# A decoder layer's banded self-attention: the row of maxima copied by ScalarE, and GpSimd's division three steps later

## The reference

```python
scores = jnp.einsum('bhtd,bhsd->bhts', q, k) / SCALE
scores = jnp.where(causal[None, None], scores, NEG_INF)
attn = jax.nn.softmax(scores, axis=-1)
mask = jnp.clip((R + z[:, :, None, None] - dist) / R, 0.0, 1.0)
attn = attn * mask
attn = attn / (attn.sum(axis=-1, keepdims=True) + 1e-08)
out = jnp.einsum('bhts,bhsd->bhtd', attn, v)
```

## Time and profile before

| what | value |
|---|---|
| device time, median of 3 runs | 3279.68 us (3276.38 to 3284.31) |
| the profiled execution | 3284.68 us |
| its span, first to last instruction | 3282.8 us |
| mean granted clock of TensorE, as a share of 2.4 GHz | 0.937 |
| PE busy | 2934.6 us (89%) |
| DVE busy | 1784.8 us (54%) |
| ACT busy | 1124.4 us (34%) |
| POOL busy | 874.1 us (27%) |

### The profile page before, as it was taken

The page is one execution under the profiler, slowest core; times in us unless marked ns, Lnnn a source line. Parts: engine busy times, 40 slices in busy tenths (PEclk is TensorE's granted clock), DMA queues, the critical chain, the costliest instruction groups (busy, mean ns, idle before and its releaser), DMA issues. The chain is left out here.

```text
span 3282.8 us, 49291 instructions
## 1 busy us (share of the span) xinstructions
PE 2934.6 (89%) x18474; PEld 1649.8 (50%) x18474; DVE 1784.8 (54%) x2008; ACT 1124.4 (34%) x2638; POOL 874.1 (27%) x730
## 2 busy tenths in 40 slices
PE   8998799999998999999998789999999787777778
PEld 6876333333333334333333678888888342332345
DVE  4355577778786878777783345555554510000038
ACT  3222444445454545444454223333333100110123
POOL 0000544444453444444353022222221000000013
PEclk9999799999999999999999799999999888878889
DMA  4553766565766565565744411112211769999954
GB/s 167 179 202 131 179 134 148 127 153 128 158 141 132 137 147 140 128 142 121 155 97 84 157 36 65 64 64 67 68 66 65 261 248 420 420 421 420 421 220 160
DMA packets 215608, 555.84 MB, mean 169 GB/s; under 512 B 31534, under 2 KB 65992, under 8 KB 178585
## 3 DMA queue, kind: packets, MB, share of 16 engines
q1 hardware_dynamic: 194649, 442.24, 38.9%
q0 software_dynamic: 13824, 100.67, 15.5%
q10 hardware_dynamic: 6976, 10.75, 0.9%
HBM read 359.87 MB, written 84.14 MB: 135 GB/s over the span
## 5 line engine op out<-in xcount | busy, mean ns | idle before, releaser
L804 ACT ACTIVATE B_e<-B_pS 128x512 f32<-128x512 f32 (+3 forms) x1280 | 614.1, 533 | 752.3 <-PE B_pS L899 430.1
L750 DVE TENSOR_REDUCE mx<-B_pM 128x4 f32<-128x2048 f32 (+2 forms) x299 | 592.1, 1980 | 311.9 <-PE B_pM L885 219.5
L694 POOL TENSOR_TENSOR B_em<-B_e,B_mask 128x512 f32<-128x512 f32 (+3 forms) x288 | 435.0, 1512 | 587.1 <-PE B_pN L938 579.5
L899 PE MATMUL B_pS<-B_qs,B_ks 97*128 97x512 f32 (+3 forms) x1280 | 503.4, 447 | 20.8 <-DMA B_qs<-q_hi 10.3
L743 DVE SCALAR_TENSOR_TENSOR B_em<-B_mask,B_e 128x1536 f32<-128x1536 f32 (+3 forms) x288 | 471.3, 1637 | 54.4 <-ACT B_e L804 52.5
L899 PEld LDWEIGHTS B_pS<-B_qs,B_ks 97*128 97x128 f32 x1280 | 226.9, 193 | 346.8 <-issue 224.9
L931 PE MATMUL B_pD<-B_em,B_ones 128*32 128x512 f32 (+3 forms) x2560 | 317.7, 569 | 18.0 <-POOL B_em L694 9.8
L938 PE MATMUL B_pN<-B_em,B_v 128*32 128x512 f32 (+3 forms) x2560 | 307.7, 552 | 0.0
L2125 PE MATMUL E_pI<-ring,hT 128*32 128x512 f32 x1024 | 184.3, 813 | 101.9 <-DMA ring<-in_L_ffn_e_W_dram 57.8
L2048 DVE TENSOR_TENSOR E_ug<-E_pT,bT 128x32 f32 x32 | 5.7, 192 | 446.5 <-PE E_pT L2135 446.5
L924 PE MATMUL B_pD<-B_e,B_tiny 128*32 128x512 f32 (+3 forms) x1792 | 203.8, 538 | 27.4 <-DMA B_e<-B_e 27.4
(11 more groups left out here) (294 smaller groups left out, 4696.5 us busy)
## 6 DMA issues: line engine op xcount, KB each, us to landing
ring<-in_L_ffn_e_W_dram SPq DMA_DIRECT2D x128, 1024.0 KB, 21.8
B_e<-B_e POOLq DMA_DIRECT2D x96, 1024.0 KB, 7.7
ring<-in_L_ffn_e_Wg_dram SPq DMA_DIRECT2D x64, 1024.0 KB, 23.6
B_ks<-k_hi SPq DMA_DIRECT2D x64, 256.0 KB, 3.9
B_qs<-q_hi SPq DMA_DIRECT2D x64, 256.0 KB, 4.5
E_xq<-xT_sc ACTq DMA_DIRECT2D x18, 512.0 KB, 10.2
ring<-x_sc SPq DMA_DIRECT2D x36, 256.0 KB, 2.7
qc<-in_x_dram SPq DMA_DIRECT2D x34, 256.0 KB, 2.7
```

The source lines that it names most:

```text
L694: nc.gpsimd.tensor_tensor(em[:, f % SLOTS_EM, mine, w0:], e[:, f % SLOTS_E, mine, w0:], mask_of(f, mine), ALU.mult).then_inc(masked_pool, 1)
L750: nc.vector.tensor_reduce(mx[:, :, qt, c], pM[:, :, 0:w], AX.X, ALU.max).then_inc(max_taken, 1)
L804: nc.scalar.activation(e[:, f % SLOTS_E, h, w0:], pS[:, h % SBANKS, w0:], ACT.Exp, scale=SCALE).then_inc(exp_ready, 1)
L899: last = nc.tensor.matmul(pS[:, h % SBANKS, w0:], ks[0:ROWS_S, kb // NT, h, kb % NT * P:(kb % NT + 1) * P], qs[0:ROWS_S, qb, h, w0:], star ...
```

## The change

The 32 copies of the transposed maxima go from DVE to ACT: `take_turned` becomes a ScalarE Copy. ACT does it in the same step as PE's transposition, between its second and third exponential, and issues the row's DMA after the fourth exponential of that step (before, in the next step between the second and the third). DVE no longer waits for the transposition there; instead its next `B_mm` waits that the last one was transposed. Two constants give the places behind a row's end: the inversion goes from 4 to 5 steps (`INVERTED`), the division from 6 to 9 (`DIVIDED`), and SP's events for the inverse and for the store move with them.

```diff
@@ constants
+INVERTED, DIVIDED = 5, 9
@@ SP's table of events
-                events += [(g0 + ENDS[qb] + 4.5, "spread", it, qb) for qb in range(BPB) if it * BPB + qb < LAST_ROW]
-                events += [(g0 + ENDS[qb] + 6.5, "out", it, qb) for qb in range(BPB)]
+                events += [(g0 + ENDS[qb] + INVERTED + 0.5, "spread", it, qb) for qb in range(BPB) if it * BPB + qb < LAST_ROW]
+                events += [(g0 + ENDS[qb] + DIVIDED + 0.5, "out", it, qb) for qb in range(BPB)]
@@ gpsimd
-                if f >= 6 and (f - 6) % STEPS in ENDS:
-                    divide(row_at(f - 6))
-            for row in range(row_at(ITS * STEPS - 5), LAST_ROW + 1):
-                divide(row)
+                if f >= DIVIDED and (f - DIVIDED) % STEPS in ENDS:
+                    divide(row_at(f - DIVIDED))
+            divide(LAST_ROW)
@@ vector, reduce_unit
                 if u % STEPS in ENDS:
                     dve.wait_ge(max_taken, u + 1)
+                    dve.wait_ge(turned, row_at(u))
@@ vector
-            def take_turned(row):
-                dve.wait_ge(turned, row + 1)
-                at_least(dve, mrow_loaded, 16 * row)
-                nc.vector.tensor_copy(mrow[:, :], pM[0:ROWS, 0, 0:P]).then_inc(mrow_ready, 1)
...
-            take_turned(0)
             dve.wait_ge(spans_loaded, 16)
             take_spans(0)
-            take_turned(1)
...
-                if (u - 1) % STEPS in ENDS and u <= ITS * STEPS:
-                    take_turned(row_at(u - 1))
...
-                if f >= 4 and (f - 4) % STEPS in ENDS:
-                    invert(row_at(f - 4))
+                if f >= INVERTED and (f - INVERTED) % STEPS in ENDS:
+                    invert(row_at(f - INVERTED))
@@ scalar
+            def take_turned(row):
+                act.wait_ge(turned, row + 1)
+                at_least(act, mrow_loaded, 16 * row)
+                nc.scalar.activation(mrow[:, :], pM[0:ROWS, 0, 0:P], ACT.Copy).then_inc(mrow_ready, 1)
...
-            row_out(0)
-            row_out(1)
+            for row in range(EARLY_ROWS):
+                take_turned(row)
+                row_out(row)
...
-                u = f - 1 + STEPS - EARLY
-                if (u - 1) % STEPS in ENDS and EARLY < u <= ITS * STEPS:
-                    row_out(row_at(u - 1))
+                u = f + STEPS - EARLY
+                turns = (u - 1) % STEPS in ENDS and EARLY < u <= ITS * STEPS
+                if turns:
+                    take_turned(row_at(u - 1))
                 if f < ITS * STEPS:
                     exps(f, (2, 3))
+                if turns:
+                    row_out(row_at(u - 1))
```

## The result

The changed kernel takes 3201.17 us (3194.32 to 3207.57, 4 runs) against 3281.41 us (3276.38 to 3284.31) of the kernel before, timed beside it: a ratio of 0.9757 with a 95% interval of 0.9727 to 0.9787. Timed again, beside later experiments, it took 3203.99 us, ratio 0.9768 (0.9739 to 0.9796). The forecast was 3200 us.

A forecast was written before the change was run, and what follows sets the result against it. PE, busy 1278 of 1385 us, was taken to bound the phase that turns rows of maxima. 36 + 17 + 9 + 27 − 9 = 80 us off 3284.7 us, less 5.0 us to the median, gave 3200 us; range 3168 to 3246.

The forecast's parts named there:

- A, the copy: PE's 42.7 us of waits for the copy of the maxima: moving it to ACT saves 36 us (27 to 42).
- B, the pairs: PE's 23.9 us of waits for DMAs adding pairs of blocks: the later division saves 17 us (0 to 21).
- the usual time to landing: Step in B: a pair's DMA lands 7.7 us after its issue.
- C, POOL's blocks: PE's 9.8 us of waits for POOL's weighted blocks: 9 us saved (0 to 10).
- D, the clock: PE's low clock behind the waits of A and B: 27 us saved (0 to 41), at 0.37 us per low us.
- E, the losses: Costs of the moves: pair DMA behind the division 4, step 14 2, steps 6 and 26 3; 9 us lost (0 to 25).
- the clock stays low: Rival: waits for B_mm at steps 5 and 25 alone keep PE's clock down; 53 us saved, 3227 us; chance 0.18.
- The sums are late anyway: Rival: PE's gain at steps 21 and 33 is lost waiting for pair DMAs; 40 us saved, 3240 us; chance 0.10.
- PE's wait stays: Rival: ACT comes to the copy as late as DVE did; only B and C act, 26 us, 3254 us; chance 0.05.
- POOL stands: Slower rival: POOL waits w at divisions, costing 24 × (w − 1), deciding from 3.6 us; 3321 us; chance 0.05.
- Nothing is counted for SP's moves: SP's moved inverse transfers and stores, now behind loads, cost nothing; without that cover the inverse would be late at the division.

The follow-up runs named there:

- late_only: Kernel before, copy still on DVE, with only the inversion and division moved to 5 and 9 steps: 3258.28 us, ratio 0.9907.
- copy_only: Changed kernel with inversion and division back at 4 and 6 steps, so only the copy moves to ACT: 3241.66 us, ratio 0.9875.
- fill_wait: Kernel before, with unused products of PE put into its waits for DVE's copy: 3263.05 us, ratio 0.9936.
- inv5_div6: Changed kernel with the division back at 6 steps, inversion still at 5: 3323.01 us, ratio 1.0124.
- inv4_div9: Changed kernel with the inversion back at 4 steps, division still at 9: 3194.75 us, ratio 0.9728.
- k_after_pairs_inv5: Changed kernel with only the four loads of k moved, to steps 37, 39, 41 and 43: 3180.19 us, ratio 0.9694.

## Why the prediction was right

The sum said 80 us, the phase gave 82.4, and the ratio's interval makes it 70 to 90 us of 3281. By the terms:

- **A, the copy: right, a little better.** 36 us were expected, of 42.7. ACT's copy takes 0.27 us, where I took 0.28, and the unit behind it waits nowhere: the 0.22 us that I left at step 33 were not there, since ACT began 0.03 us behind the transposition's end (830.82 to 830.85), where I had taken 0.16, and the unit 0.08 us behind the scores (831.29 to 831.37). All 42.7 us went. The Trainium skill, on its page "ScalarE: Activation LUTs", section "Rules for kernel authors", would keep simple elementwise work on VectorE, with a figure for bf16. This trace shows no such difference for a 16 x 128 copy in fp32: 0.27 us on ACT, 0.27 us on DVE.
- **B, the pairs: the term that was mis-sized.** 17 us were expected, 6.8 came over the whole phase (27.4 to 20.6; the stretch of the earlier trace rows shows 3.3, since it cuts the kernel before short). The 8.9 us at step 22 went, as forecast; the 11.1 at step 34 did not. The step that failed is "the pair goes out when POOL's masking is done", with "the usual time to landing": it does go out then, at 1.1 us of step 32, but lands 8.4 to 11.9 us later, because of the loads of k just ahead. late_only shows what the later places are worth alone, 13.6 us; copy_only, in which PE comes earlier, loses 3.6.
- **C, POOL's blocks: right.** 9 us expected, 7.3 came in this stretch, and what is left is one wait at the phase's start.
- **D, the clock: right.** 27 us expected; the phase shrank by 27.5 us more than PE's idle time, with 68 us less at the lower clock. The forecast priced some 73 us of it at 0.37. That price was low, 0.47 at one place and 0.40 in the mean: the 1.26 us were set against all 3.4 us at the lower clock, though it had fallen ahead of the piece measured, since the two scores ahead of it took 1.06 us (at 733.95) where the changed kernel's take 0.88 (at 711.17). At steps 5, 6, 25 and 26 low stretches stood at 15 of 15 places before and at 2 of 15 now. The reason given, that they stand behind the copy's wait, is borne out by copy_only (113 to 61 us, 4 of the 15 places left), late_only (no fall, 15 places) and fill_wait (8 places).
- **E, the losses: too high.** 9 us expected. The pair behind the division (issued at 859.84 in the earlier trace rows), for which I put 4 us, is awaited nowhere at step 36. Step 14 has its 8.2 us as before, and step 6 has 1.5 where I put 3 for steps 6 and 26. So 1.6 us were lost.

Together 42.7 + 6.8 + 7.3 + 27.5 − 1.6 = 82.7 us, against 82.4 in the phase. What B fell short of, 10 us, and C, 2, was made up by A and E, 7 each; that the sum is so close is luck in part.

Of the rivals, *the clock stays low* fell: the waits of 0.83 and 1.14 us for `B_mm` are all there, and the clock mostly stays full behind them. The rule it drew on, the Trainium skill's "TensorE: Matmul & The Clock Gate", section "HAM oscillation — how this bites in real kernels", speaks of one long gap; by it the waits for the copy, 2.0 us at most, would not matter to the clock. The runs disagree: with the copy moved and nothing else (copy_only), 51 us at the lower clock went. *The sums are late anyway* held at step 34 alone, but with another cause than the one it gave. *PE's wait stays* fell at once. *POOL stands* did not come about, since three steps more are enough for the inverse; but the mechanism is real and, where the room is missing, makes the kernel slower than before (inv5_div6). It would decide from a mean stand of 5.0 us (63 = 24 × (w − 2.4)), not 3.6.

One more term was wrong by omission. "Nothing is counted for SP's moves" named the inverse as the thing that could be late. The inverse was never late; what the moved transfers cost is seen in inv4_div9, which has them a step earlier and waits 7 us less for pairs.

**Open.** Why the pair's DMA is slow in even iterations and less so in odd ones. And what decides whether a wait brings the clock down: at the same place, behind the same wait, it stayed full in the changed kernel, as shown above, and fell in k_after_pairs_inv5. That run's timeline and a stretch of 5 us:

```profile
711.38 0.28 PE L869 MATMUL B_pM<-ident,B_mm 128*16 128x128 f32 x1 [0.85 <-DVE B_mm L754]
713.77 1.81 PE L932 MATMUL B_pD<-B_em,B_ones 128*32 128x512 f32 x8 [0.20 <-DVE B_em L743]
```
```profile
713.00:718.00 5.00, 4.79 (x24) 1.33 (x23) 2.99 (x4) 1.67 (x5) 1.44 (x2) 0.66 0.79 163
```

It fell there at 9 of the 15 places behind waits of 0.85 and 1.14 us, against 2 in the changed kernel (1 in its second profile), though PE's idle time in the phase was 16 us less. The amount of standing alone does not set it.

## What to carry to other kernels

When the engine that sets the time waits for a short instruction, look at what is ahead of that instruction in its engine's list: moving 0.27 us of work to an engine that has nothing else to do at that moment took away waits of 1 to 2 us, and the clock's fall behind them paid half as much again. When a stall on a queue goes, ask what else was passing while it lasted: the pair that POOL no longer delayed ran into loads that its delay had let go by. Bulk loads for the next iteration belong where no short transfer is awaited, behind the last pair here, and then whatever stands behind them on the same queue has to be given the room.

## What was not expected of the hardware

- A DMA that adds in place, issued 1.5 us behind 768 KB of loads from another queue, began 2.1 to 3.7 us from its issue in place of 1.4, and landed after up to 11.9 us, where it took 6.9 to 7.6 without these loads.
- POOL's division of 128 x 512 took 1.26 to 2.47 us before, and takes 1.27 to 1.30 at every one of 31 places after. All the long ones, as at 847.81 in the earlier trace rows, overlap a weighting of DVE (line 743), though not every overlap made one long. In 12 of the 17 above 1.3 us the duration is 1.13 to 1.14 us and the time of the overlap (2.40 us with 1.27 us of overlap at 847.81), as if the division stood still for so long; beside DVE's reduction alone (line 750) each took 1.27. The new place is beside a reduction nearly always, as here in the timeline of the changed kernel:

```profile
827.79 2.29 DVE L750 TENSOR_REDUCE mx<-B_pM 128x4 f32<-128x2048 f32 x1 [1.12 <-PE B_pM L882]
828.07 1.28 POOL L712 TENSOR_TENSOR B_ao<-B_num,B_inv 128x512 f32<-128x512 f32 x1
```

- Two changes that each took away idle time gave back more clock together than apart: 68 us less at the lower level against 48 (51 with the copy alone, 3 more with the places alone). Each is one execution; the second profile of the changed kernel has some 75 us less.
